# Second cross attention: values computed with the shares stationary and the context moving as a pair of halves

## The chip, the cores and the metric

One Trainium2 chip, one of its cores. The metric is the time of one execution in device microseconds. The program has five engines with queues of their own: TensorE (PE in the rows, PEld its weight loads), VectorE (DVE), ScalarE (ACT), GpSimd (POOL) and SyncE (SP, which only issues transfers here).

## What is computed

Two decoder layers over x of 8 batches of 100 rows of 512, with a context of 8 x 722 rows of 512. Each layer is self attention, cross attention and a feed-forward part, each followed by a residual sum and a layer norm. The change lies in the cross attention of the second layer and in the product behind it:

```
q = query @ Wq.T + bq;  k = key @ Wk.T + bk;  v = value @ Wv.T + bv   # hidden 1024
scores = einsum('bqh,bkh->bqk', q, k) * 64**-0.5
attn   = softmax(scores, axis=1)                 # over the 100 queries, not over the keys
out    = einsum('bqk,bkh->bqh', attn, v) @ Wo.T + bo
```

The kernel has Wk folded into the queries and Wv and Wo folded into one matrix `n1` (512 x 512), so a batch needs `scores.T = ctx @ q'`, a softmax along the free dimension, `a = shares @ ctx` (100 x 512, from 722 keys), and `a @ n1` with a bias term that comes from the sums of the shares.

## The kernel before

**The stage.** `context_columns` (L1284) treats the 8 batches one after another. The keys of a batch lie in six tiles (KT = 6) of 128 rows, the last of 82. Two copies of the context of a batch come by transfers: `ctx_ct`, with the features on the partitions, in two buffers at the top of the memory (`load_turned`, L2594), and the natural one, in `raws`, five buffers in turn: three in `shelf` and two `ctx_lent` ones that lie over xT (L685 to L699). Rows 0 and 1 of both are loaded in earlier stages.

**TensorE's order**, written out by hand: `scores(b+1)`, then `value(b)`. `scores` (L1319) makes 24 products: ct tiles stationary, the queries moving (100 columns). `value` (L1331) makes 24: for each of four column blocks of the context and each key tile, the context tile (128 x 128) is stationary and the shares `pT` (100 columns) move, so that the output is already turned (features on the partitions). Every one of them is on plain float32, and shows as two MATMUL instructions. Behind them stand six short products (L1341) that sum the shares. Then `keep_a` on ScalarE (L1364) copies the output into `xf`.

**VectorE's order** for each b: `shift(b+1)` (bias from PSUM and `x_qbk`, L1386; maximum, L1392; minus the scaled maximum, L1394), `share(b+1)` (sum, L1402; reciprocal, L1404; shares, L1406), `beside`, which is `kernel_piece`: eight chained steps (L2612 and L1066 to L1072) that quantise an eighth of the last layer's weight, and `count(b)` (L1412), a copy of the sums. ScalarE's `expo` (L1358) stands between `shift` and `share`. GpSimd adds the output bias to the eight rows of x at the stage's start (`add_bias`, L615), and has nothing else to do here.

**The last stage** (from L2621) multiplies `xf` by `n1` in plain float32 (`context_out`, L2643: four products of 512 columns, eight MATMUL instructions a batch) and adds the bias term (L2646), three batches ahead and then one for each batch; VectorE adds the residual (L2677), norms go by GpSimd (L2736, L2738, L2744), the float8 product and the last norm follow.

**Pairs.** Elsewhere the kernel splits a float32 operand into a high half, written as `float32r` by ScalarE, and a low half, the difference, also `float32r`. `times(a, b)` gives three products, high x high, high x low and low x high, each a single MATMUL instruction.

Of the kernel before, what the change touches and what calls it, by code (L numbers as in the profile page):

```python
# [14 lines left out]
ALU = mybir.AluOpType  # L15
# [8 lines left out]
P = 128  # L24
# [90 lines left out]
def program(nc, g, out):  # L115
    ctx = ExitStack()
    with ctx:
# [567 lines left out]
        RAWS = 5  # L685
# [5 lines left out]
        def load_context(sp, layer, b):  # L691

            whole = (KT - 1) * P
            landed = ctx_landed[layer][b % RAWS]
            sp.dma_start(raws[b % RAWS][:, 0:KT - 1, :],
                         g["ctx_1024"][b, 0:whole, :].rearrange("(j p) d -> p j d", p=P)).then_inc(landed, 16)
            sp.dma_start(raws[b % RAWS][0:LAST, KT - 1, :],
                         g["ctx_1024"][b, whole:S, :]).then_inc(landed, 16)
# [585 lines left out]
        def context_columns(name, qT, aT_out, scale, phase, sums_out, qbk, rows_landed, beside):  # L1284
# [4 lines left out]
            raw = raws  # L1289
            ct = turned_ahead  # L1290
            pk = sb(name + "_pk", [P, 2, KT, T], F32, phase)
            pT = sb(name + "_pT", [P, 2, KT, T], F32, phase)
            one = sb(name + "_one", [P, HD], F32, phase)
            st = sb(name + "_st", [P, 2, 3, KT], F32, phase)
            landed = ctx_landed[1]
            (zeroed, scored, shifted, peak, less, ex, sums, root, even, used, summed, counted,
             a_kept, residual) = (sem(f"{name}_{s}") for s in (
                 "zeroed", "scored", "shifted", "peak", "less", "exp", "sums", "root", "even",
                 "used", "rowsum", "counted", "a_kept", "residual"))
            with nc.Block() as block:  # L1300
                @block.sync
                def _(sp):
                    for b in range(2, B):
                        if b >= RAWS:
                            sp.wait_ge(used, b - RAWS + 1)
                        load_context(sp, 1, b)
                        sp.wait_ge(scored, 2 * (b - 1))
                        load_turned(sp, b)

                @block.tensor  # L1310
                def _(pe):
# [12 lines left out]
                    def value(b, c):  # L1324
                        if c == 0:
                            pe.wait_ge(even, b + 1)
                            pe.wait_ge(landed[b % RAWS], 32 * (b // RAWS + 1))
                            if b >= 1:
                                pe.wait_ge(a_kept, b)
# [5 lines left out]
                        if c == C - 1:  # L1335
                            mm.then_inc(used, 1)
                            if b >= 1:
                                pe.wait_ge(counted, b)
                            for j in range(KT):
                                group = j % HPC  # L1340
                                mm = nc.tensor.matmul(ps[group * HD:(group + 1) * HD, 5, 0:T], one[0:keys(j), :],  # L1341
                                                      pT[0:keys(j), b % 2, j, :], start=j < HPC, stop=j + HPC >= KT,
                                                      skip_group_check=True)
                            mm.then_inc(summed, 1)
# [9 lines left out]
                def _(act):  # L1354
                    def expo(b):
# [6 lines left out]
                    def keep_a(b):  # L1362
                        act.wait_ge(used, b + 1)
                        nc.scalar.activation(aT_out[:, :, b * T:(b + 1) * T],  # L1364
                                             ps[:, VB, 0:C * T].rearrange("p (c t) -> p c t", c=C),
                                             ACT.Identity).then_inc(a_kept, 1)

                    expo(0)
                    for b in range(B):
                        if b + 1 < B:  # L1370
# [1476 lines left out]
```

## Time and profile before

| | us |
|---|---|
| time, median of 3 (lowest, highest) | 1034.74 (1030.09, 1035.86) |
| the profiled execution's own time | 1035.91 |
| its span | 1034.1 |
| PE busy | 948.4 |
| VectorE, ScalarE, GpSimd busy | 408.1, 309.6, 180.8 |
| second cross attention | 874.3 to 965.3 |
| last stage | 965.3 to 1034.1 |

The span is the profiled execution between its first and last instruction; 1.8 us of the execution's own time lie around it. Start times in rows count from the span's start.

### The profile page before, as it was taken

The numbers are of one execution on the slowest core, as the hardware profiler recorded it, in microseconds if no ns is written. First come the engines' busy times: TensorE is split into PE (matmuls) and PEld (weight loads), VectorE is DVE, ScalarE is ACT, GpSimd is POOL, SyncE is SP. The second block draws the span as 40 slices with busy tenths as digits, with TensorE's granted clock in tenths as the row PEclk, the third lists the DMA queues.
The fourth block names the chain that finished last, engine by engine and source line by source line (L and its number), as shares of the span: only waits on it lengthen the run. The fifth ranks groups of instructions, "written<-read, shape, count | busy, mean of one in ns | idle before, by whom it ended". The sixth has DMA issues, their size and how long they took to land. (4 is left out here: it accounts for less than half of the span.)

```text
span 1034.1 us, 19172 instructions
## 1 busy us (share of the span) xinstructions
PE 948.4 (92%) x7812; PEld 747.3 (72%) x7812; DVE 408.1 (39%) x929; ACT 309.6 (30%) x821; POOL 180.8 (17%) x277
## 2 busy tenths in 40 slices
PE   4989999989999979999999999998979879999983
PEld 3887666477888335449999999996865549999531
DVE  2683444303332436001122123226257740655576
ACT  2422222122221021112222323324366622212374
POOL 4243000000000115000000000003065401200275
PEclk9999999999999989999999999997969989999995
DMA  9967000026641905139999888811040003982001
GB/s 260 382 224 249 4 2 2 10 100 204 228 190 58 334 1 181 71 87 382 365 382 326 280 278 268 274 42 54 1 152 2 2 31 128 308 261 80 1 14 50
DMA packets 72455, 162.02 MB, mean 157 GB/s; under 512 B 4131, under 2 KB 5684, under 8 KB 70320
## 3 DMA queue, kind: packets, MB, share of 16 engines
q1 hardware_dynamic: 70048, 156.54, 44.3%
q0 software_dynamic: 2320, 4.25, 1.3%
q8 instruction: 62, 1.02, 0.4%
q14 instruction: 25, 0.20, 0.1%
HBM read 128.81 MB, written 31.97 MB: 155 GB/s over the span
## 5 line engine op out<-in xcount | busy, mean ns | idle before, releaser
L1883 PE MATMUL ps<-ffn_h,ffn_w 128*128 128x128 f32 x1280 | 149.1, 275 | 0.0
L1883 PEld LDWEIGHTS ps<-ffn_h,ffn_w 128*128 128x128 f32 x1280 | 145.9, 192 | 0.0
L1883 PE MATMUL ps<-ffn_xh,ffn_w 128*128 128x128 f32 x640 | 74.9, 275 | 0.3 <-ACT ffn_xh L1917 0.3
L1883 PEld LDWEIGHTS ps<-ffn_xh,ffn_w 128*128 128x128 f32 x640 | 73.1, 192 | 0.9 <-issue 0.9
L1973 DVE TENSOR_SCALAR ffn_h<-ps,tile_bias 128x128 f32<-128x128 f32 x80 | 22.5, 344 | 122.4 <-PE ps L1883 122.4
L1931 ACT ACTIVATE ffn_y<-ffn_y 128x128 f32<-128x128 f32 x80 | 23.8, 298 | 73.9 <-DVE ffn_y L1989 73.9
L1989 DVE SCALAR_TENSOR_TENSOR ffn_y<-ps,tile_bias,ffn_gate_row 128x128 f32<-128x128 f32 x80 | 22.6, 344 | 58.0 <-PE ps L1883 57.9
L1319 PE MATMUL ps<-x_qT,ctx_ct 128*128 128x100 f32 (+1 forms) x384 | 43.1, 272 | 1.4 <-PEq L163 1.1
L1319 PEld LDWEIGHTS ps<-x_qT,ctx_ct 128*128 128x128 f32 (+1 forms) x384 | 41.7, 185 | 2.8 <-issue 2.3
L2554 POOL TENSOR_TENSOR att_e<-att_e,decay 100x400 f32<-100x400 f32 x32 | 32.7, 1033 | 50.9 <-DVE att_e L2403 50.9
L111 PE MATMUL ps<-ctx_ct,x_qT 128*100 128x210 f32 (+1 forms) x128 | 40.2, 467 | 1.0 <-DVE ctx_ct L1246 0.7
L1925 ACT ACTIVATE ffn_h<-ps,tile_bias 128x128 f32<-128x128 f32 x80 | 22.8, 368 | 41.6 <-PE ps L1883 41.6
L1170 PE MATMUL ps<-ctx_pT,shelf 128*128 128x100 f32 (+1 forms) x288 | 34.4, 275 | 0.8 <-ACT ctx_pT L1220 0.8
L111 PEld LDWEIGHTS ps<-ctx_ct,x_qT 128*100 128x100 f32 x128 | 20.6, 166 | 18.7 <-issue 17.4
L1170 PEld LDWEIGHTS ps<-ctx_pT,shelf 128*128 128x128 f32 (+1 forms) x288 | 33.3, 192 | 1.0 <-ACT ctx_pT L1220 1.0
L1331 PE MATMUL ps<-ctx_pT,shelf 128*128 128x100 f32 (+1 forms) x288 | 33.3, 275 | 0.2 <-ACT xf L1364 0.2
L1331 PEld LDWEIGHTS ps<-ctx_pT,shelf 128*128 128x128 f32 (+1 forms) x288 | 32.6, 192 | 0.5 <-issue 0.4
L2508 ACT ACTIVATE att_e<-att_e,att_mx 100x100 f32<-100x100 f32 x96 | 28.1, 366 | 15.6 <-DVE att_mx L2408 15.6
L463 POOL TENSOR_SCALAR rstd<-mean_var 100x1 f32<-100x1 f32 x8 | 3.1, 393 | 165.5 <-DVE mean_var L423 165.5
L111 PE MATMUL ps<-x_wv,xf 128*100 128x512 f32 x64 | 30.1, 620 | 1.7 <-PEq L137 1.7
L111 PE MATMUL ps<-l_ro,xf 128*100 128x512 f32 x64 | 29.8, 610 | 1.4 <-DVE xf L2421 1.4
L2643 PE MATMUL ps<-x_n,xf 128*100 128x512 f32 x64 | 29.9, 596 | 0.6 <-PEq L1300 0.6
(428 smaller groups left out, 1871.2 us busy)
## 6 DMA issues: line engine op xcount, KB each, us to landing
ffn_w<-in_L_ffn_w_dram SPq DMA_DIRECT2D x60, 1024.0 KB, 6.3
shelf<-in_ctx_dram SPq DMA_DIRECT2D x12, 1280.0 KB
expert_rows<-nothing SPq DMA_DIRECT2D x1, 14820.0 KB, 49.6
context_turned<-ctx_ct SPq DMA_DIRECT2D x8, 1444.0 KB, 8.9
ctx_ct<-context_turned SPq DMA_DIRECT2D x8, 1444.0 KB, 15.0
ctx_lent<-in_ctx_dram SPq DMA_DIRECT2D x4, 1280.0 KB
rows_own<-expert_rows SPq DMA_DIRECT2D x8, 260.0 KB, 3.0
x_wo<-in_L_xattn_Wo_dram SPq DMA_DIRECT2D x1, 2048.0 KB, 7.7
```

Of the source, the lines that this page charges most:

```text
L111: last = pe.matmul(out, a, b, start=(n == 0), stop=(n == len(products) - 1))
L1170: mm = nc.tensor.matmul(ps[:, VB, c * T:(c + 1) * T], raw[b % RAWS][0:keys(j), j, c * P:(c + 1) * P], pT[0:keys(j), b % 2, j, :], start=j ...
L1319: mm = nc.tensor.matmul(ps[0:rows_, SB + i, (j - j0) * T:(j - j0 + 1) * T], ct[b % 2][:, k, j * P:j * P + rows_], qT[:, k, b * T:(b + 1) * T],
L1331: mm = nc.tensor.matmul(ps[:, VB, c * T:(c + 1) * T], raw[b % RAWS][0:keys(j), j, c * P:(c + 1) * P], pT[0:keys(j), b % 2, j, :], start=j ...
L1883: mm = nc.tensor.matmul(acc(n)[:, m, :], w[:, n % SLOTS, k, m * P:(m + 1) * P], into[l][:, i % 2, k, :], start=k == 0, stop=k == C - 1, sk ...
L1925: nc.scalar.activation(h1[:, i % 2, m, :], acc(n)[:, m, :], ACT.Relu, bias=bsel[:, m, i, 0:1]).then_inc(h1_kept, 1)
L1931: nc.scalar.activation(y[:, i % 2, m, :], y[:, i % 2, m, :], ACT.Relu, accum_out=vT[:, m, i:i + 1]).then_inc(counted, 1)
L1973: nc.vector.tensor_scalar(h2[:, i % 2, m, :], acc(n)[:, m, :], bsel[:, m, i, 1:2], 0.0, ALU.add, ALU.max).then_inc(h2_kept, 1)
L1989: nc.vector.scalar_tensor_tensor(y[:, i % 2, m, :], acc(n)[:, m, :], bsel[:, m, i, 2:3], gate_row[:, i % 2, :], ALU.add, ALU.mult).then_in ...
L2508: ins = nc.scalar.activation(e[:, c, :], e[:, c, :], ACT.Exp, bias=mx[:, b % 2, r, c:c + 1])
L2554: nc.gpsimd.tensor_tensor(e, e, decay[:, :].unsqueeze(1).to_broadcast([T, C, T]), ALU.mult).then_inc(faded, 1)
L2643: mm = nc.tensor.matmul(ps[0:T, b % 3, :], xf[:, k, b * T:(b + 1) * T], n1[:, k, :], start=k == 0, stop=False)
```

## The change

- `value(b)` is turned round. The shares are stationary, as a pair `pp` (128 keys x 100 queries), and the context moves, as a pair of 512 columns: six key tiles times three products, all into one bank as 100 x 512.
- The halves of the context are made in the stage: ScalarE writes `raw_high` (two buffers) in four instructions a batch (two of 2 x 512 elements a partition, two of 512), GpSimd subtracts to get `raw_low` in place over the raw row, in four instructions of the same sizes. The halves of the shares: high by ScalarE (`high_of_p`), low by VectorE (`low_of_p`).
- The output is copied by ScalarE (`keep_natural`), turned by four TensorE transposes (`turn_out(b-1)`, between `scores(b+1)` and `value(b)`), and kept as a pair in `aT1` (`high_of_a` on ScalarE, `low_of_a` on VectorE).
- The natural context goes round three buffers, `own_raws`, not five. SyncE issues the turned row first, and the natural row behind a wait for `used` of three batches before.
- `n1` is split into a pair in the stage (high in one ScalarE instruction of 2048 elements ahead of `high_of_p(0)`, low in four GpSimd instructions at batches 2 and 3). GpSimd's bias additions are spread, one a batch.
- VectorE's order for each b becomes: `count(b-1)`, `shift(b+1)`, `beside(b)`, `low_of_a(b-1)`, `share(b+1)`, `low_of_p(b+1)`.
- The output product uses pairs: twelve MATMUL instructions a batch in place of eight.

```diff
-            raw = raws
+            raw = own_raws
+            raw_low = [sb_at(f"{name}_low{i}", [P, KT, D], shelf_at + 4 * KT * D * i, FR) for i in range(OWN_RAWS)]
+            raw_high = [sb_at(name + "_high0", [P, KT, D], xT_at, FR), sb(name + "_high1", [P, KT, D], FR, phase)]
...
+            PIECES = ((0, P, 0, 2), (1, P, 2, 4), (2, P, 4, KT - 1), (3, LAST, KT - 1, KT))
...
                     for b in range(2, B):
-                        if b >= RAWS:
-                            sp.wait_ge(used, b - RAWS + 1)
-                        load_context(sp, 1, b)
                         sp.wait_ge(scored, 2 * (b - 1))
                         load_turned(sp, b)
+                        if b >= OWN_RAWS:
+                            sp.wait_ge(used, b - OWN_RAWS + 1)
+                        load_context(sp, 1, b)
...
+                    def value(b):
+                        pe.wait_ge(low_p, b + 1)
+                        if b >= 1:
+                            pe.wait_ge(natural_a, b)
                         for j in range(KT):
-                            mm = nc.tensor.matmul(ps[:, VB, c * T:(c + 1) * T],
-                                                  raw[b % RAWS][0:keys(j), j, c * P:(c + 1) * P],
-                                                  pT[0:keys(j), b % 2, j, :], start=j == 0, stop=j == KT - 1,
+                            pe.wait_ge(low_raw, len(PIECES) * b + (j // 2 + 1 if j < KT - 1 else len(PIECES)))
+                            r = slice(0, keys(j))
+                            products = times(pp[r, b % 2, j, :], Pair(raw_high[b % 2], raw_low[b % OWN_RAWS])[r, j, :])
+                            for n, (p_, c_) in enumerate(products):
+                                mm = nc.tensor.matmul(ps[0:T, VB, :], p_, c_, start=j == 0 and n == 0,
+                                                      stop=j == KT - 1 and n == 2)
...
                     for b in range(B):
                         if b + 1 < B:
                             scores(b + 1)
-                        for c in range(C):
-                            value(b, c)
+                        if b:
+                            turn_out(b - 1)
+                        value(b)
+                    turn_out(B - 1)
...
+                    split(0, range(4))
                     expo(0)
+                    nc.scalar.activation(n1p.hi[:, :, :], n1[:], ACT.Identity).then_inc(high_n1, 1)
+                    high_of_p(0)
                     for b in range(B):
+                        if b:
+                            keep_natural(b - 1)
                         if b + 1 < B:
+                            split(b + 1, (0, 1))
                             expo(b + 1)
-                        keep_a(b)
+                        if b:
+                            high_of_a(b - 1)
+                        if b + 1 < B:
+                            split(b + 1, (2, 3))
+                            high_of_p(b + 1)
+                    keep_natural(B - 1)
+                    high_of_a(B - 1)
...
-                    add_bias(rows_landed, residual)
+                    def low_of_raw(b):
+                        for i, rows_, j0, j1 in PIECES:
+                            pool.wait_ge(high_raw, len(PIECES) * b + i + 1)
+                            nc.gpsimd.tensor_tensor(raw_low[b % OWN_RAWS][0:rows_, j0:j1, :], raw[b % OWN_RAWS][0:rows_, j0:j1, :],
+                                                    raw_high[b % 2][0:rows_, j0:j1, :].bitcast(F32), ALU.subtract
+                                                    ).then_inc(low_raw, 1)
+
+                    pool.wait_ge(rows_landed, 16)
+                    for b in range(B):
+                        low_of_raw(b)
+                        nc.gpsimd.tensor_tensor(x[0:T, b, :], x[0:T, b, :], bo_rows[0:T, :], ALU.add).then_inc(residual, 1)
+                        if b in (2, 3):
+                            pool.wait_ge(high_n1, 1)
+                            for m in (2 * (b - 2), 2 * (b - 2) + 1):
+                                nc.gpsimd.tensor_tensor(n1p.lo[:, m, :], n1[:, m, :], n1p.hi[:, m, :].bitcast(F32), ALU.subtract
+                                                        ).then_inc(low_n1, 1)
...
+                    low_of_p(0)
                     for b in range(B):
+                        if b:
+                            count(b - 1)
                         if b + 1 < B:
                             shift(b + 1)
+                        beside(dve, b)
+                        if b:
+                            low_of_a(b - 1)
+                        if b + 1 < B:
                             share(b + 1)
-                        beside(dve, b)
-                        count(b)
+                            low_of_p(b + 1)
+                    count(B - 1)
+                    low_of_a(B - 1)
...
-                        mm = nc.tensor.matmul(ps[0:T, b % 3, :], xf[:, k, b * T:(b + 1) * T], n1[:, k, :],
-                                              start=k == 0, stop=False)
+                        for n, (a_, w_) in enumerate(times(aT1[:, k, b * T:(b + 1) * T], n1p[:, k, :])):
+                            nc.tensor.matmul(ps[0:T, b % 3, :], a_, w_, start=k == 0 and n == 0, stop=False)
```

## Rows read from the trace of the kernel before

**Rows 1.** The page: span, and busy time of the engines

```profile
span 1034.1 us, 19172 instructions
...
PE 948.4 (92%) x7812; PEld 747.3 (72%) x7812; DVE 408.1 (39%) x929; ACT 309.6 (30%) x821; POOL 180.8 (17%) x277
```

**Rows 2.** Busy time by stage: PE, PEld, DVE, ACT, POOL, PE clock, DMA

```profile
885.40:965.30 79.90, 79.07 (x769) 76.95 (x769) 48.42 (x121) 16.08 (x50) 0.00 (x0) 1.00 0.56 186
```

**Rows 3.** Timeline of one batch of the stage: start, duration, instruction [idle before]

```profile
940.79 0.94 DVE L1386 TENSOR_TENSOR ctx_pk<-ps,x_qbk 128x500 f32<-128x500 f32 x2 [2.46 <-PE ps L1319]
...
941.28 5.52 PE L1331 MATMUL ps<-ctx_pT,shelf 128*128 128x100 f32 x48
...
942.58 0.17 DVE L1394 TENSOR_SCALAR ctx_st<-ctx_st 128x6 f32<-128x6 f32 x1
942.79 1.72 ACT L1358 ACTIVATE ctx_pk<-ctx_pk,ctx_st 128x100 f32<-128x100 f32 x6 [6.60 <-DVE ctx_st L1394]
...
945.58 0.78 DVE L1406 TENSOR_TENSOR ctx_pT<-ctx_pk,ctx_st 128x600 f32<-128x600 f32 x1
...
947.20 5.39 PE L1319 MATMUL ps<-x_qT,ctx_ct 128*128 128x100 f32 x48
...
949.24 0.25 DVE L1412 COPY x_sums<-ps 128x100 f32<-128x100 f32 x1
...
952.43 0.39 PE L1331 MATMUL ps<-ctx_pT,shelf 128*128 128x100 f32 x2
```

**Rows 4.** Timeline of the stage's start

```profile
874.34 9.85 POOL L615 TENSOR_TENSOR x<-x,bo_rows 100x512 f32<-100x512 f32 x8 [28.51 <-POOLq L163]
...
880.87 0.90 DVE L1394 TENSOR_SCALAR ctx_st<-ctx_st 128x6 f32<-128x6 f32 x1
```

**Rows 5.** Timeline of an early stage, GpSimd and VectorE

```profile
40.48 1.05 POOL L657 TENSOR_TENSOR rope_t<-rope_f,cos_q 128x400 f32<-128x400 f32 x1 [26.87 <-ACT rope_f L648]
...
41.09 0.87 DVE L676 TENSOR_TENSOR rope_t<-rope_t,sin_q 128x400 f32<-128x400 f32 x1
...
42.00 0.58 DVE L681 TENSOR_TENSOR q_roped<-rope_t,rope_t 128x400 f32<-128x400 f32 x1
```

**Rows 6.** Timeline of the last stage, GpSimd and VectorE

```profile
986.72 1.26 POOL L2762 TENSOR_TENSOR y<-x,y 100x512 f32<-100x512 f32 x1 [2.50 <-DVE y L2700]
...
987.01 1.26 DVE L2689 TENSOR_SCALAR x_quant<-x_quant 100x512 f32<-100x512 f32 x1
...
993.58 0.43 DVE L2689 TENSOR_SCALAR x_quant<-x_quant 100x512 f32<-100x512 f32 x1
```

**Rows 7.** Timeline of the second self attention: a reduction under a GpSimd instruction

```profile
784.59 2.03 POOL L2554 TENSOR_TENSOR att_e<-att_e,decay 100x400 f32<-100x400 f32 x2 [1.78 <-DVE att_e L2403]
...
785.65 0.57 DVE L2408 TENSOR_REDUCE att_mx<-att_e 100x4 f32<-100x400 f32 x1 [0.67 <-POOL att_e L2554]
```

**Rows 8.** Groups by form: a ScalarE half of 1024 elements (busy us, mean ns)

```profile
L1943 ACT ACTIVATE l_pq_hi<-l_raw_q 128x1024 fp32r<-128x1024 f32 x2 | 2.1, 1056 | 0.0
```

**Rows 9.** Timeline of PE: pair products of 512 columns, 100 stationary

```profile
87.62 0.39 PE L111 MATMUL ps<-l_wv_hi,xT_hi 128*100 128x512 f32 x1
...
89.47 0.40 PE L111 MATMUL ps<-l_wv_hi,xT_lo 128*100 128x512 f32 x1
```

**Rows 10.** Timeline of PE: end of the stage and the output product

```profile
964.14 0.54 PE L1341 MATMUL ps<-ctx_pT,ctx_one 128*32 128x100 f32 x12
965.31 3.65 PE L2643 MATMUL ps<-x_n,xf 128*100 128x512 f32 x8 [0.63 <-PEq L1300]
...
969.65 3.60 PE L2643 MATMUL ps<-x_n,xf 128*100 128x512 f32 x8
```

**Rows 11.** Timeline of PE after an idle stretch, and later

```profile
849.73 0.67 PE L111 MATMUL ps<-xT_hi,x_uz_hi 128*128 128x400 f32 x1 [2.33 <-PEq L137]
...
852.20 0.54 PE L111 MATMUL ps<-xT_lo,x_uz_hi 128*128 128x400 f32 x1
...
853.03 0.35 PE L111 MATMUL ps<-xT_lo,x_uz_hi 128*128 128x400 f32 x1
```

More of the change, by code:

```diff
@@ L1292, in context_columns @@
             pT = sb(name + "_pT", [P, 2, KT, T], F32, phase)
+            pp = Pair(*(sb(f"{name}_pT_{half}", [P, 2, KT, T], FR, phase) for half in ("hi", "lo")))
+            an = sb(name + "_a", [T, 2, D], F32, phase)
             one = sb(name + "_one", [P, HD], F32, phase)
@@ L1295, in context_columns @@
             landed = ctx_landed[1]
-            (zeroed, scored, shifted, peak, less, ex, sums, root, even, used, summed, counted,
-             a_kept, residual) = (sem(f"{name}_{s}") for s in (
+            (zeroed, scored, shifted, peak, less, ex, sums, root, even, used, summed, counted, high_p, low_p, high_raw, low_raw,
+             natural_a, flipped, a_hi, a_lo, high_n1, low_n1, residual) = (sem(f"{name}_{s}") for s in (
                  "zeroed", "scored", "shifted", "peak", "less", "exp", "sums", "root", "even",
-                 "used", "rowsum", "counted", "a_kept", "residual"))
+                 "used", "rowsum", "counted", "high_p", "low_p", "high_raw", "low_raw", "natural", "flipped", "a_hi", "a_lo",
+                 "high_n1", "low_n1", "residual"))
+            PIECES = ((0, P, 0, 2), (1, P, 2, 4), (2, P, 4, KT - 1), (3, LAST, KT - 1, KT))
+            flip_bank = lambda b: ps[:, b % 2, 0:C * T].rearrange("p (c t) -> p c t", c=C)
             with nc.Block() as block:
@@ new lines, in value @@
+                    def value(b):
+                        pe.wait_ge(low_p, b + 1)
+                        if b >= 1:
+                            pe.wait_ge(natural_a, b)
+                        for j in range(KT):
+                            pe.wait_ge(low_raw, len(PIECES) * b + (j // 2 + 1 if j < KT - 1 else len(PIECES)))
[4 more added lines that the diff above has]
+                                                      stop=j == KT - 1 and n == 2)
+                        mm.then_inc(used, 1)
+                        if b >= 1:
+                            pe.wait_ge(counted, b)
+                        for j in range(KT):
+                            group = j % HPC
+                            mm = nc.tensor.matmul(ps[group * HD:(group + 1) * HD, 5, 0:T], one[0:keys(j), :],
+                                                  pT[0:keys(j), b % 2, j, :], start=j < HPC, stop=j + HPC >= KT,
+                                                  skip_group_check=True)
+                        mm.then_inc(summed, 1)
@@ L1346, in _, with turn_out @@
+                    def turn_out(b):
+                        pe.wait_ge(natural_a, b + 1)
+                        if b >= 2:
+                            pe.wait_ge(a_lo, b - 1)
+                        for c in range(C):
+                            mm = nc.tensor.transpose(flip_bank(b)[:, c, :], an[:, b % 2, c * P:(c + 1) * P], ident[0:T, 0:T])
+                        mm.then_inc(flipped, 1)
                     scores(0)
```

63 lines of the change are left out of this document (38 added, 25 removed).

## The prediction

> **What bounds the kernel now.** I read the page first: TensorE is busy 92% of the span, VectorE 39%, GpSimd 17% [rows 1]. The busy time by stage then shows that in the stage of the change this is true to the last per cent: 79.07 of 79.9 us, at a clock of 1.00, with VectorE at 48.42 and GpSimd at nothing [rows 2]. The timeline of one batch shows the cycle: value products start at 941.28 and the next ones at 952.43, so a batch takes 11.15 us; score products begin at 947.20 [rows 3]. That is 5.9 for values and share sums and 5.2 for scores. VectorE does a batch's work in 8.7 us (940.79 to 949.49), waiting for ScalarE's exponentials inside it, and then waits 2.46 for TensorE [rows 3]. So the stage is TensorE's as long as the chain on VectorE stays under TensorE's cycle.
>
> **TensorE's part.** The 48 instructions of `value` go from 941.28 to about 946.73, 5.46 us with 0.114 each (share sums then take the rest to 947.20) [rows 3]. The new form is 18 instructions of 512 columns with 100 stationary ones. The same form starts at 87.62 and, eight instructions later, at 89.47: 0.231 each [rows 9], 4.16 us. Four transposes are added, at 0.114 an instruction about 0.5. New cycle: 5.9 - 5.46 + 4.16 + 0.5 + 5.2 = 10.3 us, 0.85 less a batch. In the last stage eight plain instructions of a product and two of the bias take 969.65 - 965.31 = 4.34 us, 0.434 each [rows 10]. Twelve at 0.231 and two at 0.434 take 3.64: 0.7 less a batch. TensorE's work is ahead of everything only at the start and at every second batch there; following made -> norm -> float8 input -> transposes, I count the first two batches and three later ones as saved, 5 x 0.7 = 3.5 us.
>
> **What is added to the others.** *ScalarE*: 1024 elements take 1.06 [rows 8], so a batch's high halves cost 1.06 + 1.06 + 0.6 + 0.6; two copies of the output and the high half of the shares 0.6 + 0.5 + 0.7 (estimates from the same row, the fixed part kept), exponentials 1.72 as before: 6.8 us, which fits. *VectorE*: to its 8.7 come `low_of_a` (400 elements with one operand in PSUM, 0.57 as a 400-element instruction [rows 5]) and `low_of_p` (600 elements, like L1406, 0.78 [rows 3]), and the wait for ScalarE's high half between shares and low half, 0.75. Against that, the 1.8 in which VectorE waited for the exponentials [rows 3] is now filled by `kernel_piece`. Chain without any disturbance: 8.7 + 0.6 + 0.8 + 0.75 - 1.8, with the gaps 9.3. That would fit under 10.3. *GpSimd*: eight additions of 512 elements take 9.85, 1.23 each [rows 4]; 400 elements take 1.05 [rows 5], so 0.0016 to 0.002 us an element, and 1024 take 2.05 to 2.46 (twice the short one); I take 2.3. A batch needs 2.3 + 2.3 + 1.2 + 1.2 for the low halves and 1.2 for the bias: 8.3 us, at batches 2 and 3 with two more instructions 10.7. By itself that would be hidden too.
>
> **The collision.** GpSimd and VectorE are not independent. In the first batch of this stage the six-column TENSOR_SCALAR L1394 takes 0.90, and 0.17 in a later one [rows 3, 4]. It began at 880.87 while GpSimd was adding; the additions are 1.23 apart from 874.34, one ends at 881.73, and it ended at 881.77. The same in an early stage: GpSimd's instruction ends at 41.53, VectorE's two-operand TENSOR_TENSOR of 41.09 ends at 41.96, 0.87 long where its like takes 0.58 [rows 5]. And in the last stage: 1.26 in place of 0.43, ended 0.29 behind the end of GpSimd's 986.72 [rows 6]. So an instruction of this kind waits for GpSimd's running one and then needs its own time less some 0.14. A reduction of 0.57 ran unharmed inside two GpSimd instructions [rows 7]. The Trainium skill (SBUF — State Buffer, § SBUF: two separate sides, and its practical consequences) says it as a rule: TENSOR_SCALAR in its fast mode, and anything with two SBUF inputs, is fully blocked by a GpSimd instruction that started first, and blocks one likewise; a reduction is not. By its list all eight steps of `kernel_piece` would be concerned, and the traces agree where they show it. The same skill (GPSIMD Reference, § 3.1) gives 4497 ns for 2048 elements, with which a batch's low halves would be 6.8 us and not 7.0, and the batch below 15.0 and not 15.2.
>
> Exposed on VectorE per batch: L1394, the eight steps (2.9 us together, 946.36 to 949.24), L1406 and `low_of_p`: eleven instructions, 4.6 us, some 3.1 without the part that a wait hides [rows 3]. GpSimd's 8.3 us exclude them: 11.4 to 12.9 us a batch even if nothing else left a gap, which is more than the 10.3 of TensorE and the 11.15 of before. The steady batch, walked through, time 0 at the end of `low_of_p(b)`:
> - ScalarE has copied `natural(b-1)` by -0.2 and makes halves 0 and 1 of row b+1 by 0.9 and 1.9. GpSimd's piece 0 runs 0.9 to 3.2.
> - VectorE: count to 0.3, bias to 1.25, maximum to 2.05, then L1394 waits to 3.25. Piece 1 goes 3.25 to 5.55; the first step of `kernel_piece` waits behind it, to 5.75. Exponentials 3.3 to 5.0, turned output's high half to 5.55, halves 2 and 3 to 6.15 and 6.8.
> - Two more steps to 6.4, then GpSimd's piece 2, one step, piece 3, one step, the bias addition, one step (to 10.45), two steps to 11.25. `low_of_a` 11.85, sum and reciprocal 12.85, L1406 13.65, the high half on ScalarE 14.4, `low_of_p` 15.2.
>
> A batch takes 15.2 us: 9.3 plus 6.2 of waits, less what the waits hide. TensorE, at 10.3, now waits. At batches 2 and 3 two more GpSimd instructions come between steps, 1.85 more each.
>
> **The stage.** `low_of_p(0)` ends at about 12.5 us behind the stage's start (scores 4.85, shift, L1394 blocked to 7.25, exponentials 9.0, the high half of `n1`, two 1024s, to 11.0, high half of the shares, low half). The next comes 14.0 later (no `low_of_a` yet, one piece already done), then 17.05 twice and 15.2 four times: 121.4. `value(7)` takes 0.5 + 4.2 at the high clock. TensorE has then been idle for most of 10 us. After 2.33 us of idle time the products at 849.73 to 852.20 took 0.54, and 0.35 from 853.03 on [rows 11]: the lower of the two clocks (1.2 GHz, then 2.4). I add 2 us. The tail is copy, transposes, high half, low half and the block's end, 0.6 each with its handover: 2.9, where it was 1.2 between the last sums at 964.14 and 965.31 [rows 10]. The stage is then 131 us long. Before it is 91.0 (874.34 to 965.31) [rows 4, 10]. **Sum: +40 - 3.5 = +36.5.** On the profiled execution's own 1035.9 (span 1034.1 and 1.8 around it) that is 1072.4; its time stands 1.2 over the median of 1034.7, on which the forecast is 1071.
>
> **At nothing** I cost: the ten or so new waits of TensorE; the transfers (2.9 MB a batch as before; the natural row waits for `used` and the row behind it waits on SyncE with it, but with 15 us a batch there is room; under 10.3 it would be tighter); and TensorE's lower clock inside batches, since 5 us of its 15 are idle, which covers it.
>
> **Rivals.**
> - *VectorE keeps the port through its chained steps* (GpSimd doesn't get in between two of them). No row shows which of two waiting engines goes next in a chain with gaps of 0.03 us. Then steps end at 8.5, pieces 2 and 3 run under `low_of_a` and the sums, and a batch takes 13.3: `low_of_p(7)` at 107, the stage 116, time 1035 + 25 - 3 = 1057.
> - *No exclusion that matters, TensorE stays the bound*: faster. First value at 12.0, six cycles of 10.3, then 9.3 and the tail 3.1: 86 against 91; with the last stage -8, 1027. It decides if GpSimd's pieces hold VectorE up by less than 1 us a batch. For it: GpSimd is idle here in all batches but the first, so only one instruction of this stage shows the wait. Against it: rows of three stages show the wait, each to within 0.05 us or so of the same sum.
> - *Perfect packing*: the port is busy without a gap, 11.4 a batch: `low_of_p(7)` at 97, time 1035 + 13 - 4 = 1044.
> - *Worse*: the low clock makes TensorE's 10.3 into 15 and over in each batch, or a row lands late: 1085.
>
> **Numbers.** Forecast 0.50, VectorE keeps the port 0.22, perfect packing 0.10, worse 0.05, TensorE stays the bound 0.10, and 0.03 for a balance that ends near no change. Range 1038 to 1084: below it lies the fast rival, above it the worst. The forecast's own range is 1060 to 1082. No change means within 0.5%, 5 us, about what a measurement can tell here: faster 0.10, same 0.04, slower 0.86.
>
> **What would show it.** Right: L1394 at 1 us and the steps of `kernel_piece` at 0.4 to 2.3 where they took 0.29 to 0.43; GpSimd busy for over 70 us in the stage; TensorE waiting for `low_of_p` some 5 us a batch; value products 0.231 apart; the output product starting every 3.6 us. Wrong: steps at their old lengths under GpSimd's pieces, or a stage under 100 us with TensorE busy throughout.

## The result, and the profile after

The changed kernel takes 1073.34 us (median of 4 runs, 1065.88 to 1075.70) against 1035.30 of the kernel before on the same chip (4 runs, 1030.09 to 1036.51): ratio 1.037, 95% interval 1.032 to 1.042. The forecast was 1071, range 1038 to 1084, slower with 0.86.

The first lines of the page after, then the busy time by stage. The columns are those of [rows 2]; the stretches are the attention stage, its part behind the first low half of the shares, and the last stage.

```profile
span 1071.4 us, 18952 instructions
...
PE 952.3 (89%) x7636; PEld 744.9 (70%) x7636; DVE 464.9 (43%) x945; ACT 344.4 (32%) x870; POOL 246.3 (23%) x313
```

```profile
873.60:1002.40 128.80, 96.93 (x656) 78.29 (x656) 108.84 (x146) 52.11 (x105) 74.44 (x44) 0.85 0.40 139
885.90:1002.40 116.50, 86.17 (x560) 67.86 (x560) 103.80 (x137) 44.04 (x93) 66.08 (x39) 0.84 0.39 135
1002.40:1071.40 69.00, 45.05 (x176) 25.14 (x176) 43.17 (x82) 38.54 (x72) 41.13 (x70) 0.81 0.08 24
```

The attention stage is 128.8 us long where it was 91.0, and the last stage 69.0 where it was 68.8. TensorE had 79.07 of 79.9 us filled [rows 2]; now it has 86.17 of 116.5, and VectorE has 103.80, in which the time that its instructions stand waiting for GpSimd's is counted as busy. The transfers have come down to 0.39 of their engines from 0.56, so they are not what is short.

One steady batch after, the counterpart of [rows 3]: start, duration, instruction.

```profile
932.88 0.79 DVE L1477 TENSOR_TENSOR ctx_pT_lo<-ctx_pT,ctx_pT_hi 128x600 fp32r<-128x600 f32 x1 [0.77 <-ACT ctx_pT_hi L1392]
...
933.39 0.93 PE L1358 MATMUL ps<-ident,ctx_a 100*128 100x100 f32 x4 [3.84 <-ACT ctx_a L1398]
...
934.36 4.70 POOL L1427 TENSOR_TENSOR ctx_low<-shelf,ctx_high 128x1024 fp32r<-128x1024 f32 x2 [5.07 <-ACT ctx_high L1378]
...
935.43 1.32 DVE L1457 TENSOR_SCALAR ctx_st<-ctx_st 128x6 f32<-128x6 f32 x1
...
936.67 2.54 DVE L2695 TENSOR_SCALAR k_quant<-kernel,s_k 128x256 f32<-128x256 bf16 x1
...
939.25 0.29 DVE L1067 TENSOR_SCALAR k_quant<-k_quant 128x256 int32<-128x256 int32 x1
...
939.50 2.56 POOL L1427 TENSOR_TENSOR ctx_low<-shelf,ctx_high 128x512 fp32r<-128x512 f32 x2 [0.44 <-ACT ctx_high L1378]
939.57 1.37 DVE L1068 TENSOR_SCALAR k_quant<-k_quant 128x256 f32<-128x256 f32 x1
...
940.98 1.37 DVE L1069 TENSOR_TENSOR k_quant<-k_quant 128x256 f32<-128x256 f32 x1
...
942.03 1.45 POOL L1434 TENSOR_TENSOR x<-x,bo_rows 100x512 f32<-100x512 f32 x1
942.38 1.38 DVE L1070 TENSOR_TENSOR k_quant<-k_quant 128x256 f32<-128x256 f32 x1
...
947.85 0.78 DVE L1477 TENSOR_TENSOR ctx_pT_lo<-ctx_pT,ctx_pT_hi 128x600 fp32r<-128x600 f32 x1 [0.77 <-ACT ctx_pT_hi L1392]
```

A batch takes 947.85 - 932.88 = 14.97 us, and TensorE's idle 3.84 ahead of the transposes is where it waits for the copy that stands behind the high half of the shares on ScalarE. In the whole stage it waited 28.9 us for this copy, and never for GpSimd's low half of the context. The delay is made on VectorE: L1457 takes 1.32 where it took 0.17, the first matrix step (L2695) 2.54, and three more 1.37 or 1.38 each where they took 0.29 to 0.43. Each of them ends 0.03 to 0.3 behind the end of a GpSimd instruction (the two pieces from 934.36 take 4.70 / 2 = 2.35 each, so the first ends at 936.7, and L1457 at 936.75). The two 512-column pieces and the addition of GpSimd alternate with VectorE's three steps, one by one.

The end of the stage, from the timeline of TensorE:

```profile
996.53 0.63 PE L1341 MATMUL ps<-ctx_high,ctx_pT_hi 128*100 128x512 f32 x1
...
997.49 0.39 PE L1341 MATMUL ps<-ctx_high,ctx_pT_hi 128*100 128x512 f32 x1
...
1000.43 0.57 PE L1358 MATMUL ps<-ident,ctx_a 100*128 100x100 f32 x4 [0.22 <-ACT ctx_a L1398]
1002.47 0.45 PE L2729 MATMUL ps<-x_n_hi,x_aT_hi 128*100 128x512 f32 x1 [1.47 <-PEq L1308]
```

Value products take 0.39 and follow 0.23 apart at the upper clock, and take 0.63 and follow 0.43 apart at the lower (1.2 GHz), in which `value(7)` ran until 997 after 9.8 us without work (granted clock 0.50 from 993.2 to 996.9, and 1.00 from 997.3 on). The last lines show the tail of turning and splitting.

### The profile page after: what moved, and what is told of

The parts are those of the page before. It is cut to its first block and busy times, and to the rows that moved or that the text cites. A ratio compares the mean times of both kernels' runs of the same rounds, so it can differ in the third digit from the quotient of the medians.

```text
span 1071.4 us, 18952 instructions
## 1 busy us (share of the span) xinstructions
PE 952.3 (89%) x7636; PEld 744.9 (70%) x7636; DVE 464.9 (43%) x945; ACT 344.4 (32%) x870; POOL 246.3 (23%) x313
## 5 line engine op out<-in xcount | busy, mean ns | idle before, releaser
L1427 POOL TENSOR_TENSOR ctx_low<-shelf,ctx_high 128x1024 fp32r<-128x1024 f32 (+2 forms) x32 | 58.1, 1838 | 69.8 <-ACT ctx_high L1378 69.7
L1171 PE MATMUL ps<-ctx_pT,shelf 128*128 128x100 f32 (+1 forms) x288 | 34.4, 275 | 0.8 <-ACT ctx_pT L1221 0.8
L1171 PEld LDWEIGHTS ps<-ctx_pT,shelf 128*128 128x128 f32 (+1 forms) x288 | 33.3, 192 | 1.0 <-ACT ctx_pT L1221 1.0
L1358 PE MATMUL ps<-ident,ctx_a 100*128 100x100 f32 x32 | 6.3, 341 | 28.9 <-ACT ctx_a L1398 28.9
L1205 ACT ACTIVATE ctx_ct<-ps 128x512 f32<-128x512 f32 x24 | 14.2, 598 | 51.1 <-PE ps L1140 43.6
```

Source lines behind the costliest of these rows:

```text
L1171: mm = nc.tensor.matmul(ps[:, VB, c * T:(c + 1) * T], raw[b % RAWS][0:keys(j), j, c * P:(c + 1) * P], pT[0:keys(j), b % 2, j, :], start=j ...
L1205: nc.scalar.activation(ct[b % 2][:, :, j * P:j * P + keys(j)], tile_of(b, j), ACT.Identity).then_inc(ct_act, 1)
L1427: nc.gpsimd.tensor_tensor(raw_low[b % OWN_RAWS][0:rows_, j0:j1, :], raw[b % OWN_RAWS][0:rows_, j0:j1, :], raw_high[b % 2][0:rows_, j0:j1, ...
```

## The experiments

Ten kernels ran, in three groups (1 to 4, 5 to 8, 9 and 10), each on another chip. The kernel before, run beside each, had a median of 1035.92, 1034.89 and 1035.31. Its own runs spread over 1029.9 to 1038.5, and in the profiled executions the attention stage begins anywhere between 868.9 and 877.4 us, with the same code ahead of it in most of them; the lengths of the two stages are therefore given beside each time. "Matrix steps" are `kernel_piece`.

### 1. The matrix steps in the stage before

On top of the changed kernel:

```diff
                     for n, (emit, view, dst, bias, scale) in enumerate(jobs):
+                        if beside is not None and n < B:
+                            beside(dve, n)
                         dve.wait_ge(hi_done, n + 1)
...
-                        beside(dve, b)
                         if b:
                             low_of_a(b - 1)
...
+                      + project(m1p, xT, qT, bias=lambda m: aux[:, m:m + 1]), sync=first_turned, beside=kernel_piece)
```

> The changed kernel with the kernel matrix's steps (4.9 us of VectorE work a batch before) taken out of the attention stage: VectorE does them one batch at a time in the stage just before (849 to 874 us), in which its row shows 0.00 us busy. The mathematics is unchanged. Theory (VectorE and GpSimd take turns on what they share, and the matrix steps are the chained two-operand instructions that pay for it with 1.3 us each): with them gone VectorE keeps some 6 us of work a batch beside GpSimd's 9.3, TensorE's cycle of 10.3 us sets the batch or is missed by a turn of 1 us at most; stage 86 to 92 us, kernel 1029 to 1038. Rival (the longer chain scores, exponentials, shares, high half, low half, value, and the waits between four engines set the batch): the chain is as long as before, so 14 to 15 us a batch and 1062 or more. Rival (the steps only change their place): what the steps cost is paid in the earlier stage instead, 8 x 4.9 = 39 us, and the kernel stays at 1070.

Measured: 1052.78 us (1052.18 to 1053.20), ratio 1.017, interval 1.013 to 1.021; attention stage 107.8 us, last stage 67.5. That is 20.5 us less than the changed kernel, where the theory gave back 35 to 44 and the first rival at most 11: neither range was met. (The steps take 2.9 us a batch in the kernel before, not the 4.9 of the expectation.) The second rival fell, since the attention stage begins at 875.3 us, only 1.7 later than in the changed kernel. The timeline shows what was left:

```profile
909.50 0.78 DVE L1457 TENSOR_REDUCE ctx_st<-ctx_pk 128x6 f32<-128x600 f32 x1
909.65 2.56 POOL L1440 TENSOR_TENSOR x_n_lo<-x_n,x_n_hi 128x512 fp32r<-128x512 f32 x2
910.31 6.57 DVE L1459 TENSOR_SCALAR ctx_st<-ctx_st 128x6 f32<-128x6 f32 x1
912.15 4.70 POOL L1429 TENSOR_TENSOR ctx_low<-shelf,ctx_high 128x1024 fp32r<-128x1024 f32 x2
916.91 1.72 ACT L1386 ACTIVATE ctx_pk<-ctx_pk,ctx_st 128x100 f32<-128x100 f32 x6 [7.02 <-DVE ctx_st L1459]
...
939.78 4.10 DVE L1459 TENSOR_SCALAR ctx_st<-ctx_st 128x6 f32<-128x6 f32 x1
```

An instruction on 128x6 elements, whose own time is 0.17 us [rows 3], took 6.57. It stood through four GpSimd instructions, from 909.65 to 916.85, and was let in at the end of none of the first three; ScalarE's exponentials started 0.03 behind its end. In the changed kernel the same instruction got in at the first end each time. The exclusion here costs more than one instruction's length, which no row of before had shown. Two instructions right ahead of it were not held up by GpSimd: the bias (L1451, one operand in PSUM) took 0.83 from 908.63 and the maximum 0.78, under an addition of GpSimd that ran from 907.85 to 909.69 and the one after it.

### 2. GpSimd's work made tiny

On top of the changed kernel:

```diff
-                            products = times(pp[r, b % 2, j, :], Pair(raw_high[b % 2], raw_low[b % OWN_RAWS])[r, j, :])
+                            products = times(pp[r, b % 2, j, :], Pair(raw_high[b % 2], raw_high[b % 2])[r, j, :])
...
-                            nc.gpsimd.tensor_tensor(raw_low[b % OWN_RAWS][0:rows_, j0:j1, :], raw[b % OWN_RAWS][0:rows_, j0:j1, :],
-                                                    raw_high[b % 2][0:rows_, j0:j1, :].bitcast(F32), ALU.subtract
+                            w_ = 8
+                            nc.gpsimd.tensor_tensor(raw_low[b % OWN_RAWS][0:rows_, j0:j1, 0:w_], raw[b % OWN_RAWS][0:rows_, j0:j1, 0:w_],
+                                                    raw_high[b % 2][0:rows_, j0:j1, 0:w_].bitcast(F32), ALU.subtract
```

> The changed kernel with GpSimd's subtractions for the low half of the context cut to 8 of 512 columns; the value product takes the high half a second time in place of the low half, so the low half of the context is left out of the result. All instructions, waits and matmuls stay; only GpSimd's 8 to 9 us of work a batch become under 1 us. Theory (the turns with GpSimd cost VectorE its time): matrix steps fall from 1.37 back to 0.35 us or less, batch 10.3 to 11.2 us set by TensorE, stage 85 to 91, kernel 1029 to 1037. Rival (VectorE's or ScalarE's own added work and the chain of waits cost it, GpSimd does not): batch 13 or more, kernel 1055 or more.

Measured: 1036.96 us (1028.72 to 1038.58), ratio 1.001, interval 0.998 to 1.004. The profiled execution, an early-starting one of 1028.76, has an attention stage of 91.8 us and a last one of 66.1:

```profile
869.00:960.80 91.80, 86.02 (x656) 71.46 (x656) 64.78 (x146) 52.62 (x105) 23.61 (x44) 0.96 0.57 195
```

```profile
902.61 0.17 DVE L1458 TENSOR_SCALAR ctx_st<-ctx_st 128x6 f32<-128x6 f32 x1
902.69 0.35 DVE L2696 TENSOR_SCALAR k_quant<-kernel,s_k 128x256 f32<-128x256 bf16 x1
...
903.73 0.42 DVE L1069 TENSOR_TENSOR k_quant<-k_quant 128x256 f32<-128x256 f32 x1
```

Every instruction and every wait of the change is still there; VectorE's small multiplication and its matrix steps are back at their own times, and VectorE is busy 64.78 us in place of 108.84. The slowdown of the stage is therefore the time in which GpSimd's work of a batch and VectorE's exclude each other. That GpSimd's work is simply too long for a batch is no rival: TensorE never waited for it in the changed kernel, and experiments 5 and 8 keep it whole and have stages of 93.3 and 92.9 us.

The last four low halves of the shares came 10.3 us apart: TensorE's cycle, as the prediction has it. The longer chain of waits costs something only at the end, where `value(7)` has no scores ahead of it:

```profile
950.70 0.93 PE L1358 MATMUL ps<-ident,ctx_a 100*128 100x100 f32 x4 [3.00 <-ACT ctx_a L1398]
```

### 3. The output product in pairs, alone

On top of the kernel before. The edit also splits `n1` (high half on ScalarE, low half in four GpSimd instructions at the stage's start) and takes three context buffers. `low_of_a` reads the output from PSUM, so that the next `value` waits for it.

```diff
-                        nc.scalar.activation(aT_out[:, :, b * T:(b + 1) * T],
+                        nc.scalar.activation(aT_out.hi[:, :, b * T:(b + 1) * T],
...
                         beside(dve, b)
                         count(b)
+                        low_of_a(b)
...
-                        mm = nc.tensor.matmul(ps[0:T, b % 3, :], xf[:, k, b * T:(b + 1) * T], n1[:, k, :],
-                                              start=k == 0, stop=False)
+                        for n, (a_, w_) in enumerate(times(aT1[:, k, b * T:(b + 1) * T], n1p[:, k, :])):
+                            nc.tensor.matmul(ps[0:T, b % 3, :], a_, w_, start=k == 0 and n == 0, stop=False)
```

> The kernel before with the output product in pairs alone (high and low half of the attention output and of n1 kept, three single-pass products in place of one of full precision, three context buffers in place of five); values as before. The prediction's term: 0.7 us saved in each of five batches, last stage 68.8 - 3.5 = 65.3 us, kernel about 1032. What the changed kernel's trace suggests: the first five output products save 2.3 to 3.2 us, TensorE then runs out of work sooner, its granted clock falls to the lower level, and the float8 products after it take 1.95 instead of 1.07 us; last stage 68 to 69.5 us, kernel 1034 to 1037. Attention stage in both: within 1.5 us of 91.0, as VectorE's added 0.9 us a batch and GpSimd's four steps have room.

Measured: 1045.18 us (1035.35 to 1048.41), ratio 1.008, interval 1.005 to 1.012; attention stage 98.7 us in the profiled execution (1038.23), last stage 68.8. The last stage gained nothing, as the changed kernel's trace suggested. The attention stage and the time fell out of both expectations. In the profiled execution the stage is longer in one place:

```profile
954.95 0.25 DVE L1424 COPY x_sums<-ps 128x100 f32<-128x100 f32 x1
955.12 0.56 DVE L1388 TENSOR_TENSOR x_aT_lo<-ps,x_aT_hi 128x400 fp32r<-128x400 f32 x1
...
955.83 9.92 PE L1332 MATMUL ps<-ctx_pT,shelf 128*128 128x100 f32 x48 [2.85 <-DVE x_aT_lo L1388]
```

The batches are 11.16 apart, as before. But `value(7)` has no scores ahead of it, waited 2.85 us for VectorE to read the bank behind the matrix steps, and then ran its 48 instructions in 9.92 us, where the values before it took 5.52. The granted clock from 955.8 to 965.7 is 0.54, so the wait of 2.9 us cost 4.4 more through the clock. The kernel's median lies 7 us above this profiled execution, whose attention stage begins early, at 868.9 us, where it begins at 874.3 in the kernel before; six of the ten executions took 1044 to 1048.4, and no trace shows one of them. The changed kernel copies the output first and reads the copy, and has no such wait.

### 4. The gaps of the last stage filled

On top of the changed kernel:

```diff
+                def fill(n):
+                    for _ in range(n):
+                        nc.tensor.matmul(ps[0:T, 7, :], identB[:, 0:T], kq[:, 0:D], start=True, stop=True)
...
                 for b in range(B):
+                    fill({2: 7, 4: 9, 5: 0, 6: 22, 7: 4}.get(b, 0))
                     turn(b)
```

> The changed kernel with matmuls of which nothing is used in the gaps of the last stage ahead of the turns of batches 2, 3, 6 and 7 (7, 9, 22 and 4 of 512 columns in bf16), so that TensorE has work until the turn can start. Result unchanged. Theory (the lower granted clock ate the 3.5 us that the output product saves): all float8 products take 1.07 us, the last stage falls from 69.0 to 65 to 67 us, kernel 1069 to 1071 against 1073 of the changed kernel. Rival (the last stage is set by other engines, the clock is only seen there): last stage 68.5 to 69.5. Rival (the added matmuls themselves are late): over 70.

Measured: 1067.78 us (1066.87 to 1070.88), ratio to before 1.032, interval 1.028 to 1.036, where the changed kernel had 1.037. Last stage 65.1 us in place of 69.0, at a clock of 0.94 in place of 0.81. TensorE at the float8 product behind the turn of the fifth and the seventh batch in the changed kernel, then this one's last stage by the busy time, and its product behind the turn of the seventh:

```profile
1040.67 0.35 PE L2740 MATMUL ps<-identB,xq 100*128 100x100 bf16 x4 [2.34 <-POOL xq L2842]
1042.14 1.95 PE L111 MATMUL ps<-kernel,xqT 128*100 128x512 bf16 x4 [0.26 <-ACT xqT L2886]
...
1054.57 0.52 PE L2740 MATMUL ps<-identB,xq 100*128 100x100 bf16 x4 [5.27 <-POOL xq L2842]
1056.04 1.95 PE L111 MATMUL ps<-kernel,xqT 128*100 128x512 bf16 x4 [0.95 <-ACT xqT L2886]
```

```profile
1000.60:1065.70 65.10, 49.09 (x218) 28.16 (x218) 42.53 (x82) 38.09 (x72) 40.97 (x70) 0.94 0.09 26
```

```profile
1050.42 0.34 PE L2740 MATMUL ps<-identB,xq 100*128 100x100 bf16 x4
1051.50 1.07 PE L111 MATMUL ps<-kernel,xqT 128*100 128x512 bf16 x4 [0.73 <-ACT xqT L2891]
```

(The gaps filled are those ahead of the turns of batches 2, 4, 6 and 7, counted from 0; the text above says 3 for 4.) In the changed kernel four of these products took 1.95; here all take 1.07. Work whose result nobody reads shortened the stage by 3.9 us, as the theory has it. The time fell by 5.6, to 1.2 under the theory's range; 2.6 of that is no effect of the edit on the last stage, as the attention stage of this execution began at 871.0 and that of the changed kernel's at 873.6.

### 5. The small multiplication on ScalarE

On top of experiment 1:

```diff
-                        dve.wait_ge(peak, b + 1)
-                        nc.vector.tensor_scalar(st[:, b % 2, 1, :], st[:, b % 2, 0, :], -scale, None,
-                                                ALU.mult).then_inc(less, 1)
...
+                        act.wait_ge(peak, b + 1)
+                        nc.scalar.activation(st[:, b % 2, 1, :], st[:, b % 2, 0, :], ACT.Identity, scale=-scale).then_inc(less, 1)
                         act.wait_ge(less, b + 1)
```

> The kernel with the matrix steps moved to the earlier stage (1052.8 us), in which the 128x6 multiplication by the scale (own time 0.17 us) waited 3.17 to 6.57 us under GpSimd's instructions in seven of eight batches and held back ScalarE's exponentials; here ScalarE does that multiplication itself. Result unchanged. Theory (what is left of the slowdown there is that one wait on what VectorE and GpSimd share): batches fall from 12.3 and 14.7 us to TensorE's 10.3 to 11.0, attention stage from 107.8 to 90 to 96 us, kernel 1035 to 1041. Rival (the turn only passes to the next two-operand instruction of VectorE, the multiplication of the shares): batch 11.8 or more, kernel 1046 or more.

Measured: 1039.59 us (1035.74 to 1041.81), ratio 1.004, interval 1.003 to 1.006; attention stage 93.3 us, all in the theory's ranges. Moving eight instructions of 0.17 us from VectorE to ScalarE took 13 us off (the ratios to the kernel before, each on its own chip, are 1.017 and 1.004). The timeline shows that the rival also has a part:

```profile
934.09 3.25 DVE L1470 TENSOR_TENSOR ctx_pT<-ctx_pk,ctx_st 128x600 f32<-128x600 f32 x1
```

The multiplication of the shares, own time 0.78 [rows 3], is now caught for 2.47 to 3.88 in four of the eight batches. It costs little, since TensorE still has scores and values to work on: in the whole stage it waited 4.1 us for the output's copy and 0.8 for the low half of the shares, and these low halves come 10.3 us apart on average, TensorE's cycle. (For the waits of experiment 1 the expectation says seven of eight batches; it was six.)

The Trainium skill (Perfetto Trace Analysis, § Optimizing Scalar/DVE Operations) says that some operations can be done by ScalarE as well as by VectorE, and that moving operations between VectorE and GpSimd might not help, because they share a read port. Experiments 1 and 5 agree with the first, 1052.8 against 1039.6 us; no run here moves an operation between VectorE and GpSimd.

### 6. What decides whether VectorE is passed over

On top of experiment 1, GpSimd's addition in another place:

```diff
                                                     ).then_inc(low_raw, 1)
+                            if i == 1:
+                                nc.gpsimd.tensor_tensor(x[0:T, b, :], x[0:T, b, :], bo_rows[0:T, :], ALU.add).then_inc(residual, 1)
...
                         low_of_raw(b)
-                        nc.gpsimd.tensor_tensor(x[0:T, b, :], x[0:T, b, :], bo_rows[0:T, :], ALU.add).then_inc(residual, 1)
```

> The same kernel (matrix steps earlier, the 128x6 multiplication on VectorE) with one edit: GpSimd does its residual addition of each batch between the second and the third piece of the context, where it stands idle 2.8 us for ScalarE, instead of right ahead of the next batch's first piece. Result unchanged. Theory A (VectorE gets in at the end of a GpSimd instruction that began after an idle time, and is passed over once GpSimd has gone from one instruction to the next unopposed): the 128x6 multiplication waits 1.1 to 1.4 us in most batches instead of 4.1 and 6.6, kernel 1034 to 1044. Theory B (whether it is passed over is not a matter of what ran before): it still waits 4.1 us, to the end of the second piece; kernel 1048 to 1053.

Measured: 1045.74 us (1040.72 to 1048.49), ratio 1.011, interval 1.007 to 1.015; attention stage 100.5. The time lies between the ranges of the two theories. A batch in which GpSimd's first piece now starts from idle:

```profile
946.63 1.13 DVE L1460 TENSOR_SCALAR ctx_st<-ctx_st 128x6 f32<-128x6 f32 x1
```

```profile
945.33 4.74 POOL L1429 TENSOR_TENSOR ctx_low<-shelf,ctx_high 128x1024 fp32r<-128x1024 f32 x2 [1.11 <-ACT ctx_high L1380]
```

In the last three of the batches the wait is 1.13 to 1.15 us, to the end of the first piece, where it was 4.1 in experiment 1. In batches 2 to 4, where another GpSimd instruction still ran right ahead of the piece, it is 4.38, 5.33 and 5.33. Theory A holds for these, but not without exception: in the first batch GpSimd had gone from one instruction to the next unopposed and VectorE was let in after 0.6 us all the same, and the 5.33 ended while GpSimd still had an addition to do. What exactly decides stays open.

### 7. The filled gaps in the kernel before

> The kernel before with matmuls of which nothing is used ahead of the turns of the last two batches of the last stage (14 and 4 of 512 columns in bf16). Result unchanged. Before, the float8 products of those two batches take 1.95 instead of 1.07 us at the lower granted clock. Theory (the clock costs the kernel before too, but less than the changed one): last stage 68.8 to 67 to 67.5 us, kernel 1033.5 to 1035. Rival (no gain at this end): 1035.5 to 1036.5.

The edit is `fill` of experiment 4 in the kernel before, with `{6: 14, 7: 4}`. Measured: 1035.71 us (1030.63 to 1038.12), ratio 1.001, interval 0.998 to 1.003. The last stage is 67.6 us in the profiled execution (clock 0.95), 1.2 less than before, with the last two float8 products at 1.07. The time shows nothing of it and lies in the rival's range: an effect of this size is below what 12 runs tell here.

### 8 to 10. The edits together

Experiment 8 joins experiments 1, 4, 5 and 6. Experiment 9 leaves the last batch's matrix steps beside `value(7)` and puts those of two other batches ahead of VectorE's first wait in the earlier stage. Experiment 10 also moves GpSimd's four subtractions for `n1` behind its last piece:

```diff
-                        if b in (2, 3):
+                        if b == B - 1:
                             pool.wait_ge(high_n1, 1)
-                            for m in (2 * (b - 2), 2 * (b - 2) + 1):
+                            for m in range(C):
```

> The changed kernel with the matrix steps in the earlier stage, the 128x6 multiplication on ScalarE, GpSimd's addition between pieces two and three, and the filled gaps of the last stage: the candidate that should beat both. Result unchanged. Theory: attention stage 90 to 95 us (TensorE's 10.0 to 10.6 a batch and a start and end that are longer than before's), last stage 65 to 66 instead of 68.8; kernel 1030 to 1036, against 1035.9 of the kernel before. Rival (ScalarE's 6.5 us a batch and the chain of waits from scores to the low half leave more than TensorE's cycle): batch 11.2 or more, kernel 1038 or more.

> The kernel of all three edits and filled gaps, with seven of the eight matrix steps in the earlier stage (two of them ahead of VectorE's first wait) and the eighth beside the last value product. Result unchanged. In that kernel the earlier stage ended at 877.0 us, on VectorE's last step, while ScalarE was done at 875.9 and in the kernel before at 873.9; attention stage 92.9 and last stage 65.1 against 91.0 and 68.8. Theory (the 1.7 us won in those two stages were lost again in the earlier one): the earlier stage ends 1.5 to 3 us sooner, kernel 1031.5 to 1033.5 against 1034.8 of the same without this edit and 1034.9 of the kernel before. Rival (the start of the attention stage varies by 5 us from run to run whatever stands there, and nothing is to be had): 1034 to 1035.5.

> The same, with GpSimd's four subtractions for the low half of n1 behind its last piece of context instead of in batches 2 and 3 (low half of the shares 14.4 us after the one before there, 8.9 to 10.7 us in the other batches). Result unchanged. Theory: TensorE waited 3.3 us at its longest in that batch, and 4.3 us in all, for ScalarE's copy of the attention output; with GpSimd's 5 us there gone, 2 to 3.5 us of this come back: attention stage 89.5 to 91, kernel 1029 to 1031.5, faster than the kernel before by 0.3 to 0.6%. Rival (that long batch is caught up by the short one after it, as TensorE runs behind anyway): within 0.7 us of the kernel without this edit.

| | median (lowest, highest), us | ratio, 95% interval | attention stage | last stage |
|---|---|---|---|---|
| 8 | 1034.77 (1032.82, 1037.29) | 1.0007 (0.9988, 1.0025) | 92.9 | 65.1 |
| 9 | 1034.39 (1029.24, 1037.16) | 0.9986 (0.9964, 1.0007) | 93.4 | 65.3 |
| 10 | 1034.42 (1028.91, 1035.88) | 0.9985 (0.9965, 1.0004) | 91.4 | 66.7 |

The stages of experiment 10, in the columns of [rows 2]:

```profile
874.20:965.60 91.40, 84.94 (x656) 70.63 (x656) 53.12 (x82) 54.07 (x113) 79.40 (x44) 0.98 0.58 195
965.60:1032.30 66.70, 50.69 (x218) 29.10 (x218) 42.50 (x82) 38.08 (x72) 41.03 (x70) 0.92 0.09 25
```

The slowdown is gone in all three, and they are some 39 us faster than the changed kernel; none is faster than the kernel before by more than its measurement can tell. Experiment 8 met its theory in both stages and in the time, but did not beat the kernel before. The theories of 9 and 10 asked for 1031.5 to 1033.5 and for under 1031.5, and got neither; for both the rival's value was met. In 10 the attention stage did get 1.5 to 2 us shorter, and the last stage was 1.4 longer in the same execution. Whether there are 1 or 2 us in them can't be read from these runs.

## Why the prediction was right, and where it was not

**The collision: right, each step within 0.25 us.** The low half of the shares of the first batch ended 12.3 us after the stage's start (predicted 12.5); the next came 13.98 later (14.0), then 16.89 twice (17.05), then 14.96 on average for four (15.2), so that the last one ended at 119.9 (121.4). The eight matrix steps ended 11.2 us into the batch (11.25). Experiment 2 shows the cause, not only the fit: with GpSimd's large instructions short and everything else in place, the stage is 91.8 us and not 128.8. One sign came out smaller than told: TensorE waited 1.8 to 3.9 us in each of the batches ahead of the last and not some 5, since for a part of all these `value`s but one it ran at the lower clock (0.43 apart). The prediction had that at nothing because idle time covers it, and it did.

**The rival "VectorE keeps the port"** fell: GpSimd got in between each two of VectorE's chained steps that it had work for (939.50 to 943.8). **"TensorE stays the bound"** is what experiments 2, 5 and 8 to 10 turned the kernel into: 91.4 to 93.4 us a stage. Its 86 us were not reached in any. In experiment 2 the first value came 11.9 us into the stage (12.0 in the rival) and the cycles took 10.3 (10.3). The end took some 5 us more than the rival has: TensorE waited 3.0 us ahead of `value(7)`, and this then took 6.7 us and not 4.2, at a granted clock of 0.60. So with the collision all but gone the new form of `value` is worth nothing in this stage, against 91.0.

**The end of the stage.** Sized 9.6 us from the last low half to the output product (0.5 + 4.2 + 2 + 2.9), measured 8.96. The 2 us for the clock were a guess of the right size: `value(7)` took 5.8. The stage: 131 predicted, 128.8 measured.

**The step that failed is the last stage's "5 x 0.7 = 3.5 us".** The product itself was sized rightly: it starts every 3.65 us where it started every 4.29, and the turn of the third batch came 24.1 us into the stage, not 25.8. Then the gain shrank: the turn of the fifth at 38.2 and 38.9, that of the seventh at 52.1 and 51.9. TensorE was idle sooner and longer, 1.67, 2.34 and 5.27 us ahead of three turns, and after each the float8 product took 1.95 us instead of 1.07; before, this happened only in the last two batches. With the gaps filled the last stage is 65.1 us with pairs (experiment 4) and 67.6 without (experiment 7); without filling it is 69.0 and 68.8. So the term is 2.5 us where the clock is held up, and nothing where it is not, each read from one profiled execution. Experiment 3 showed the same nothing with the output product alone.

**The sum.** +37.8 in the attention stage (predicted +40), +0.2 in the last one (-3.5), -0.7 ahead of it (0): two errors of opposite sign, of 2.2 and 3.7 us. In the profiled execution that makes 1073.3 us for 1072.4, and in the medians 1073.3 for 1071. So close a number is in part luck, as the two errors cancel; the collision, which makes nearly all of it, is not.

## What to carry to other kernels

Before giving GpSimd work because it is idle, look at whom it will run beside: VectorE's TENSOR_SCALAR instructions, and those with two operands that both lie in SBUF (and neither in PSUM, where TensorE's products go), wait for it, and one of 0.17 us can wait for several in a row; a small instruction that others wait for belongs on ScalarE. Work taken off TensorE in a stage where it then stands idle can come back as a slower remainder, so price such a saving with the clock that the stage is granted.

## What the runs showed of the hardware that was not expected

- **Passing over.** A waiting VectorE instruction is not always let in at the end of GpSimd's running one. L1457 of the changed kernel was, in all eight batches (0.60 to 1.36 us); the same instruction in experiment 1 waited 3.17, 6.57, 6.54, 4.10, 4.08 and 4.08 us in six of eight, through two to four instructions. The Trainium skill (SBUF — State Buffer, § SBUF: two separate sides) says that whoever starts first has the shared pair for the whole instruction; the rows agree for each single instruction. Who comes next when both have work queued is what experiments 1 and 6 leave open.
- **It goes both ways.** GpSimd's 512-column addition takes 1.45 us beside VectorE's steps (942.03) and 1.23 alone [rows 4].
- **Idle time costs more than its length.** 2.85 us without work cost `value(7)` of experiment 3 another 4.4 at the lower clock, and matmuls that compute nothing gained 3.9 us in experiment 4.
